# A Fourier block on one core: groups taken in twos, with their 64-row matmuls in one stretch

## What is computed

```
xf  = rfft2(x, axes=(H, W), norm="ortho")        # 128 x 65 frequencies, 768 channels = 8 blocks of 96
o1r = relu(xr @ w1[0] - xi @ w1[1] + b1[0])      # per block, complex weights 96 x 96
o1i = relu(xi @ w1[0] + xr @ w1[1] + b1[1])
o2r = o1r @ w2[0] - o1i @ w2[1] + b2[0]
o2i = o1i @ w2[0] + o1r @ w2[1] + b2[1]
out = irfft2(softshrink(o2r + i o2i, 0.01)) + x
```

## Time and profile before

| | |
|---|---|
| median of three runs | 5099.5 us |
| span of the profiled execution | 5094.2 us |
| what lies around the span, against the median | 5.3 us |
| TensorE busy | 98% |
| VectorE, ScalarE, GpSimd busy | 75%, 59%, 28% |
| one unit's layers, of 32 | 95.3 us (2107.73 to 2203.05) |
| granted clock of TensorE, mean | 0.993 |

### The profile page before, as it was taken

The page is one execution under the profiler, slowest core; times in us unless marked ns, Lnnn a source line. Parts: engine busy times, 40 slices in busy tenths (PEclk is TensorE's granted clock), DMA queues, the critical chain, the costliest instruction groups (busy, mean ns, idle before and its releaser), DMA issues.

```text
span 5094.2 us, 113221 instructions
## 1 busy us (share of the span) xinstructions
PE 4981.3 (98%) x40000; PEld 4673.3 (92%) x40000; DVE 3816.7 (75%) x6159; ACT 2996.3 (59%) x5409; POOL 1436.3 (28%) x905
## 2 busy tenths in 40 slices
PE   6999999999999999999999999999999999999997
PEld 6999999999999999999999999999999999999996
DVE  5777777777777777777777777777777777777876
ACT  4555655556655566555566555665556655556653
POOL 3033223332123332233321333312333123332220
PEclk8999999999999999999999999999999999999998
DMA  5044423444323443234442344432344323444233
GB/s 114 12 94 105 98 59 69 91 105 105 68 57 87 105 105 87 56 81 94 105 105 52 70 90 105 106 70 62 79 105 106 86 61 78 92 105 105 61 73 72
DMA packets 1699712, 430.24 MB, mean 84 GB/s; under 512 B 1698848, under 2 KB 1698976, under 8 KB 1699104
## 3 DMA queue, kind: packets, MB, share of 16 engines
q1 hardware_dynamic: 1696768, 421.83, 37.5%
q10 hardware_dynamic: 2336, 0.59, 0.1%
HBM read 220.84 MB, written 201.33 MB: 83 GB/s over the span
## 4 chain that ended last, share of the span: by engine, by line
PE 96%; DVE 2%; issue 1%; SPq 1%; ACT 0%; DMA 0%; DVEq 0%; ACTq 0%
PE psum L807 15%; PE psum L778 14%; PE psum L822 14%; PE psum L760 13%; PE psum L849 13%; PE psum L832 9%; PE psum L790 7%; PE psum L859 3%; PE psum L860 3%; PE psum L861 3%; DVE mixed L655 1%; SPq L387 1%; DVE spectrum L628 0%; PE psum L840 0%; PE psum L839 0%
## 5 line engine op out<-in xcount | busy, mean ns | idle before, releaser
L655 DVE COPY mixed<-psum 128x768 f32<-128x768 f32 (+1 forms) x512 | 477.4, 932 | 700.0 <-PE psum L790 700.0
L541 ACT ACTIVATE sums_high<-psum 128x512 fp32r<-128x512 f32 x768 | 459.2, 599 | 731.3 <-PE psum L849 731.2
L807 PEld LDWEIGHTS psum<-mats,mixed 128*128 128x128 f32 x6272 | 744.0, 191 | 121.2 <-issue 113.1
L807 PE MATMUL psum<-mats,mixed 128*128 128x128 f32 x6272 | 841.8, 283 | 0.0
L778 PE MATMUL psum<-w_whole,whole 128*128 128x192 f32 x4160 | 782.3, 330 | 40.9 <-ACT whole L482 11.4
L822 PE MATMUL psum<-w2t,hidden 128*128 128x192 f32 x4160 | 771.7, 328 | 0.0
L849 PE MATMUL psum<-mats,spectrum 128*128 128x128 f32 x6144 | 743.7, 275 | 3.1 <-DVE spectrum L663 1.6
L760 PE MATMUL psum<-mats,x 128*128 128x128 f32 x6144 | 704.9, 277 | 33.6 <-DVE x L582 17.8
L760 PEld LDWEIGHTS psum<-mats,x 128*128 128x128 f32 x6144 | 696.0, 193 | 40.9 <-issue 23.0
L778 PEld LDWEIGHTS psum<-w_whole,whole 128*128 128x128 f32 x4160 | 673.3, 197 | 60.6 <-issue 33.7
L849 PEld LDWEIGHTS psum<-mats,spectrum 128*128 128x128 f32 x6144 | 714.5, 192 | 4.1 <-DVE sums_low L701 2.0
(11 more groups left out here) (76 smaller groups left out, 7800.7 us busy)
## 6 DMA issues: line engine op xcount, KB each, us to landing
x<-x SPq DMA_DIRECT2D x736, 192.0 KB, 2.9
out<-x SPq DMA_DIRECT2D x736, 192.0 KB, 2.5
x<-x SPq DMA_DIRECT2D x736, 64.0 KB, 2.6
out<-x SPq DMA_DIRECT2D x736, 64.0 KB, 2.2
x<-x SPq DMA_DIRECT2D x32, 144.0 KB, 2.7
out<-x SPq DMA_DIRECT2D x32, 144.0 KB, 2.3
w2t<-L_conv_w SPq DMA_DIRECT2D x124, 36.0 KB, 1.8
x<-x SPq DMA_DIRECT2D x64, 48.0 KB, 2.4
```

Of the source, the lines that this page charges most:

```text
L655: copied = dve.tensor_copy(mixed[s % 2][:, 0:k], both_b(s)[:, 0:k])
L807: last = pe.matmul(out[tile], flat[:, tile * SIZE:(tile + 1) * SIZE], mat(FH), start=True, stop=True)
```

## The change

The groups are taken in twos: round j (ten of them) has the even group e = 2j and the odd group o = 2j + 1. TensorE's order in a full round is now, with e' and o' the groups of the round before and o'' the odd one before that: 128-row row transform of o', 128-row second layer of o'', column transform of e', 128-row row transform of e, column transform of o', 128-row second layer of e', and then the 64-row stages in one stretch: row transform of e, second layer of e', second layer of o', row transform of o.

So an odd group's sums are opened by its 64-row matmuls and closed by the 128-row ones of the next round, an even group's the other way round; `b_done` and `d_done` go with the one that closes, and the waits for `b_copied` and `seeded` with the one that opens. An odd group's 64-row row transform now waits for the copy of the even group ahead of it, which uses the same banks. ScalarE's and VectorE's orders follow. VectorE's unfold steps are cut in halves of 640 or 768 elements, sixteen for a unit, and four of these or of the sign flips stand in each round from the first on (`spare`), one ahead of each of the two copies and one behind it or behind the seed. `unfolded` comes with the last of four halves. ScalarE's gather is split in two functions; in round 0 it gathers group 1's halved part ahead of the whole one. Behind the last unit the unfold runs as sixteen steps.

The core of the diff (the `hide`, `exceed`, `mix`, `hide_middle`, `shrink` and `seed` functions hold the old bodies unchanged):

```diff
+ROUNDS = NS // 2 + 2
+def even_group(j):
+    return 2 * j if 0 <= 2 * j < NS else None
+def odd_group(j):
+    return 2 * j + 1 if 0 <= 2 * j + 1 < NS else None
...
+                for j in range(ROUNDS):
+                    if j == 0:
+                        gather_halved(1)
+                        gather_whole(1)
+                    if j > 0 and odd_group(j) is not None:
+                        act.wait_ge(b_done, n * NS + 2 * j)
+                        gather_whole(odd_group(j))
+                    if even_group(j - 1) is not None:
+                        hide(even_group(j - 1))
+                    if odd_group(j - 2) is not None:
+                        exceed(odd_group(j - 2))
+                    if j > 0 and odd_group(j) is not None:
+                        gather_halved(odd_group(j))
+                    if odd_group(j - 1) is not None:
+                        hide(odd_group(j - 1))
+                    if j == ROUNDS - 1:
+                        act.wait_ge(flip_done, n + 1)
+                        act.activation(U[:, 0:BLOCK, SIZE + 2:].rearrange("p c k -> p k c"), bank_flip,
+                                       ACT.Copy).then_inc(flip_copied, 1)
+                    if even_group(j - 1) is not None:
+                        exceed(even_group(j - 1))
+                    if even_group(j + 1) is not None:
+                        act.wait_ge(b_done, n * NS + (2 * j + 1))
+                        gather_whole(even_group(j + 1))
+                        gather_halved(even_group(j + 1))
...
             def unfold_step(n, par, k):
-                x_unit, (lo, hi) = xs[par], PIECES[k // 2]
+                p, what = divmod(k, 4)
+                x_unit, (lo, hi) = xs[par], PIECES[p]
+                lo, hi = ((lo, lo + 5), (lo + 6, hi))[what % 2]
                 up, down = x_unit[:, lo:hi + 1, :], mirrored(x_unit, lo, hi)
                 if k == 0:
                     dve.wait_ge(f_added, n * NF + NF)
                     dve.wait_ge(f_late_added, n * LATE + LATE)
                 even, odd = x_unit[:, 0, BLOCK:], x_unit[:, MIDDLE, BLOCK:]
-                if k % 2 == 0:
+                if what < 2:
                     if k == 0:
                         dve.tensor_tensor(even, even, odd, ALU.add)
                     dve.tensor_tensor(up, up, down, ALU.add).then_inc(unfold_even, 1)
                 else:
-                    dve.wait_ge(unfold_even, n * NP + (k // 2 + 1))
-                    if k == 1:
+                    dve.wait_ge(unfold_even, n * (2 * NP) + (2 * p + what - 1))
+                    if k == 2:
                         dve.scalar_tensor_tensor(odd, odd, -2.0, even, op0=ALU.mult, op1=ALU.add)
-                    dve.scalar_tensor_tensor(down, down, -2.0, up, op0=ALU.mult, op1=ALU.add).then_inc(unfolded, 1)
+                    done = dve.scalar_tensor_tensor(down, down, -2.0, up, op0=ALU.mult, op1=ALU.add)
+                    if what == 3:
+                        done.then_inc(unfolded, 1)
...
+                def spare(k):
+                    if k < 4 * NP and not first:
+                        unfold_step(n - 1, 1 - par, k)
+                    if 4 * NP <= k < 4 * NP + W_SIGNS and not last:
+                        prepare_step(m + par, 1 - par, k - 4 * NP)
+                for j in range(ROUNDS):
+                    if 0 < j:
+                        spare(4 * j - 4)
+                    if odd_group(j - 1) is not None:
+                        mix(odd_group(j - 1))
+                    if 0 < j:
+                        spare(4 * j - 3)
+                    if even_group(j - 1) is not None:
+                        hide_middle(even_group(j - 1))
+                    if odd_group(j - 2) is not None:
+                        shrink(odd_group(j - 2))
+                    if odd_group(j - 1) is not None:
+                        seed(odd_group(j - 1))
+                        hide_middle(odd_group(j - 1))
+                    if 0 < j:
+                        spare(4 * j - 2)
+                    if even_group(j) is not None:
+                        mix(even_group(j))
+                    if even_group(j - 1) is not None:
+                        shrink(even_group(j - 1))
+                    if even_group(j) is not None:
+                        seed(even_group(j))
+                    if 0 < j:
+                        spare(4 * j - 1)
...
             def stage_b_whole(par, n, s):
+                opens = s % 2 == 0
                 if s == 0:
                     pe.wait_ge(w_negated, (n + 1) * W_SIGNS)
                     pe.wait_ge(f_added, n * NF)
                     pe.wait_ge(early_gathered, (n + 1) * 3)
-                elif s >= 2:
+                elif opens:
                     pe.wait_ge(b_copied, n * NS + (s if s > 2 else 1))
                 pe.wait_ge(whole_gathered, n * NS + (s + 1))
                 for k in columns(s):
-                    pe.matmul(bank_b(s, k), whole[s % 2][:, k // 2, :, k % 2], w1_whole[par][:, :, :].rearrange("p r o -> p (r o)"),
-                              start=k % 2 == 0, stop=False, skip_group_check=True)
+                    last = pe.matmul(bank_b(s, k), whole[s % 2][:, k // 2, :, k % 2], w1_whole[par][:, :, :].rearrange("p r o -> p (r o)"),
+                                     start=opens and k % 2 == 0, stop=not opens, skip_group_check=True)
+                if not opens:
+                    last.then_inc(b_done, 1)
             def stage_b_halved(par, n, s):
+                opens = s % 2 == 1
                 if s == 0:
                     pe.wait_ge(first_halved, n + 1)
                 else:
+                    if opens and s > 1:
+                        pe.wait_ge(b_copied, n * NS + s)
                     pe.wait_ge(halved_gathered, n * (NS - 1) + s)
                 for i in range(2):
                     for y in range(2):
                             rows = slice(y * HALF, (y + 1) * HALF)
                             last = pe.matmul(bank_b(s, i + 2 * y), halved[s % 2][rows, :, i],
                                              w1_halved[par][rows, :, :].rearrange("p r o -> p (r o)"),
-                                             start=False, stop=True, skip_group_check=True)
-                last.then_inc(b_done, 1)
+                                             start=opens and i == 0, stop=not opens, skip_group_check=True)
+                if not opens:
+                    last.then_inc(b_done, 1)
...
             def stage_d_outer(par, n, s):
+                ends = s % 2 == 1
                 pe.wait_ge(relu_done, n * (2 * NS) + (2 * s + 1))
-                pe.wait_ge(seeded, n * NS + (s + 1))
+                if not ends:
+                    pe.wait_ge(seeded, n * NS + (s + 1))
                 for k in columns(s):
                     if k == 2:
                         pe.wait_ge(relu_done, n * (2 * NS) + (2 * s + 2))
-                    pe.matmul(sums_d(s, k), hidden[s % 2][:, k // 2, k % 2], w2_tile(par, slice(0, SIZE), 2 * (k // 2)),
-                              start=False, stop=False, skip_group_check=True)
+                    last = pe.matmul(sums_d(s, k), hidden[s % 2][:, k // 2, k % 2], w2_tile(par, slice(0, SIZE), 2 * (k // 2)),
+                                     start=False, stop=ends, skip_group_check=True)
+                if ends:
+                    last.then_inc(d_done, 1)
             def stage_d_middle(par, n, s):
+                ends = s % 2 == 0
                 pe.wait_ge(middle_done, n * NS + (s + 1))
+                if not ends:
+                    pe.wait_ge(seeded, n * NS + (s + 1))
                 for i in range(2):
                     for y in range(2):
                         if i + 2 * y in columns(s):
                             rows = slice(y * HALF, (y + 1) * HALF)
                             last = pe.matmul(sums_d(s, i + 2 * y), middle[s % 2][rows, i], w2_tile(par, rows, 1),
-                                             start=False, stop=True, skip_group_check=True)
-                last.then_inc(d_done, 1)
+                                             start=False, stop=ends, skip_group_check=True)
+                if ends:
+                    last.then_inc(d_done, 1)
...
             def layers(par, n):
-                for s in range(NS + 2):
-                    if s < NS:
-                        stage_b_whole(par, n, s)
-                    if s == NS:
+                for j in range(ROUNDS):
+                    if j == 1:
+                        stage_b_whole(par, n, 1)
+                    if j == ROUNDS - 1:
+                        stage_d_outer(par, n, odd_group(j - 2))
+                    if j > 1 and odd_group(j - 1) is not None:
+                        stage_b_whole(par, n, odd_group(j - 1))
+                    if j < ROUNDS - 1 and odd_group(j - 2) is not None:
+                        stage_d_outer(par, n, odd_group(j - 2))
+                    if even_group(j - 1) is not None:
```

(60 more changed lines are left out.)

100 lines of the change are left out of this document (34 added, 66 removed).

## The result

The change makes the kernel slower: median 5130.19 us (four runs, 5125.64 to 5134.33) against 5099.41 (four runs), ratio 1.0056, 95% interval 1.0041 to 1.007. The forecast was 5076, 0.5% faster. It missed by 54 us, and on the wrong side. (The span of the changed kernel's profiled execution is 5126.1 beside a time of 5127.99, so 1.9 us lie around a span; most of the 5.3 that the forecast added were differences between executions.)

What follows compares the result with a forecast made beforehand. TensorE's own queue bounds the kernel. Per unit: -3.5 us for nine visits, -0.55 for old waits, +3.35 for new ones, net -0.7; times 32 some -23, so 5099.5 becomes 5076 us; 8 in 10 range 5040 to 5108.

Steps and rivals of the forecast that it cites:

- What bounds the kernel: Whole kernel: the chain that ended last runs through TensorE for 96%, so only time on TensorE's own queue counts.
- the price of a visit: TensorE's change from 128-row to 64-row matmuls and back: 0.39 us in all, nine fewer a unit, 3.5 us.
- The estimate of 0.33: TensorE's change to 64-row matmuls and back, two drains: 0.33 us by the skill page, 96 us for those removed.
- The new round: TensorE's walk through two groups in the new order: 10.9 us without waits, where two groups took 11.29.
- the third rival: Each of the four 64-row stages pays at its border, so nothing is saved and waits stay: 5189 us, chance 0.03.
- The waits one by one: New TensorE waits in the rounds of a unit, listed from largest to smallest: sum 3.35 us, bounds 1.9 to 4.0.
- the copy costs the last stage its lead: Rounds 3 to 7, odd group's 64-row row transform: loads wait for the even group's copy, 0.09 us each, 0.45 in all.
- The row transform of group 4 in round 2: Round 2: waits 0.70 us for group 3's copy, behind excess, shrink, seed and two unfold halves on VectorE.
- the row transform of group 5: Round 2, 64-row: waits 0.41 us for group 4's copy, since group 2's second layer is half as long.
- The second rival: VectorE's copy of the even group comes late every round and becomes the bound: slower, 5143 us at 0.3 a round, chance 0.08.
- column transform of group 1: 1.16: Round 1: TensorE waits 1.16 us for VectorE's bias of group 0, behind seed, 32-element op, unfold halves and copies.
- the flips in round 6: Sign flips ahead of VectorE's copy: weighed in round 5 only, up to 1.7 us long where 1.0 is free, 0.1 us.

Runs made afterwards that it cites:

- experiment 4: The change with the even group's 64-row row transform put ahead of the 128-row second layer, two stretches of 64-row stages in rounds 1 to 8: 5216.5 us.
- experiments 5 and 6: Unfold and GpSimd's halving cut to one row, in the kernel before (5088.7 us) and in the change with sign flips moved behind the odd copy (5014.8 us).
- experiments 1, 2 and 8: The change with GpSimd's halving cut to one row (5078.0 us); with spare steps a round later (5070.9 us); with unfold halves, flips and a relu re-placed (5036.2 us).

## Why the prediction was wrong

**What bounds the kernel,** and the price of a visit, were right. 0.39 us by the timeline of before; adding one a round (experiment 4) cost 0.39 less the 0.10 of the copy's lost lead, and nine visits less with light chores gave 74 us net (experiments 5 and 6) where the walk gave 75. The estimate of 0.33 from the Trainium skill (TensorE: Matmul & The Clock Gate, Single matmul latency) is under what the traces show, 0.39.

**The new round** was right: 11.02 us for 10.99. The free border between two second layers, which the third rival doubted, is there.

**The waits one by one:** where no op of VectorE is held, a unit takes 94.62 us for 94.6. That the copy costs the last stage its lead came as walked. The row transform of group 4 in round 2 starts 0.71 us late and loses its lead, 0.8 for 0.7; the row transform of group 5 starts 0.32 late and loses its lead, 0.4 for 0.4. The second rival (0.08, 5143) came nearest: a held unfold half or sign flip is in it. Its place was wrong. It had the held op ahead of the even group's copy, for which the last 64-row stage waits, and that stage cost no more than forecast in rounds 3 to 7.

**The step that failed** is the first of the new waits, "column transform of group 1: 1.16". In the unheld units it measures 1.14 (a start 1.04 us late and the lost lead), in the 25 others 2.5. I priced each VectorE op by its length where it stood before, 0.18 us for the 32-element op, and never asked what else ran at its new place. The unfold moved from 12 us to 4 us behind the unit's start, into GpSimd's halving, and the op was held for 1.4 us. The trace had the sign: the flips' lengths, from 0.2 to 1.73 us for the same op, which I put down as a spread of one op at one place (0.1 us in round 5, "an estimate") and did not explain; and one of 5.25 us at the first unit, which no row of mine showed. Had I asked what made them long, GpSimd's timeline beside them would have answered, and the same question put to the unfold's new place would have given 1.37 us in all units but the loop's first ones: 34 us, enough to turn the sign of a walked gain of 23.

The Trainium skill, SBUF — State Buffer, section SBUF: two separate sides, has this as a rule: the pair of ports that VectorE and GpSimd share is an exclusive lock, taken for a whole instruction by whichever starts first, and VectorE needs it for an op in a two-port mode or, against a GpSimd op that reads SBUF, for one with two SBUF inputs. The runs agree: the unfold's addition (two inputs in SBUF) and the flips were held to the end of GpSimd's op, copies with one side in PSUM were not. It was a rule against this change, and I did not weigh it.

**The second failure follows from the first.** A wait of 2.2 us on TensorE cost more than its length: in 8 units the clock was at 0.52 behind it, 1.6 us more each. At 0.9 us and less (experiments 1, 2 and 8) no unit had that in round 1. I had no row with such a wait in mind, though the trace of the kernel before shows it in units 4 and 20. TensorE's timeline of unit 4, where the granted clock is 0.51 from 698.5 to 702.0:

```profile
697.50 1.94 PE L778 MATMUL psum<-w_whole,whole 128*128 128x192 f32 x8 [2.02 <-ACT whole L494]
```

**A third, small:** the flips in round 6. The prediction weighed them only in round 5, at 0.1 us a unit; two stand together ahead of a copy at the turn to round 6, and cost 12 us.

**The range** was too narrow for this. It took each wait as up to a fifth larger; the largest doubled. So the mechanism of the walk held, one of its terms had the wrong size by a hold it did not look for, and the sum, a small difference of two large terms, changed its sign with it.

## What to carry to other kernels

When a step is moved, ask of its new place what runs there on the engines that share something with it, and don't take its old length along: here an op of VectorE on SBUF operands lasted until GpSimd's op ended. A spread in the lengths of one form of instruction is a question to answer before summing. And where a regrouping shortens the slack of an in-order queue, place the chores anew: here the same regrouping is 0.6% slower or 1.2% faster, by the places of sixteen unfold halves and six sign flips (with one relu moved too).

## What the runs showed of the hardware

- An add of 32 elements on VectorE whose operands lie in SBUF took 1.55 us instead of 0.18 while GpSimd's 5.31 us op was under way, and a sign flip 5.25 us instead of 0.21; both are recorded as busy time. Copies between SBUF and PSUM, 0.95 us, were not longer in the same stretch.
- Behind a wait of 2.2 us in an otherwise full queue, TensorE's clock was granted at 0.52 in 8 of 25 units of one execution, in 5 of another and in 15 with more visits to the 64-row form (experiment 4); behind waits of up to 0.9 us at that place in none.
- A change between 128-row and 64-row matmuls costs 0.2 us each way; a border between 64-row stages of different banks nothing.
